# Score columns and biases from small products, and first and last six turns in an order of their own, in a two-layer graph attention kernel

## The reference

```python
Wh = jnp.matmul(h, W)                       # layer A; B has 4 heads of 128, C one of 256
e_i = jnp.einsum('bnf,f->bn', Wh, a1)
e_j = jnp.einsum('bnf,f->bn', Wh, a2)
e = jax.nn.leaky_relu(e_i[:, :, None] + e_j[:, None, :], negative_slope=ALPHA)
e = jnp.where(adj == 0, MASK_VAL, e)
attention = jax.nn.softmax(e, axis=2)
h_prime = jnp.matmul(attention, Wh)
...
x = _layernorm(x + _L0_gnn_ref(x, adj, L0_gnn_W, L0_gnn_a), axis=-1)
x = _layernorm(x + _L1_gnn_ref(adj, x, ...), axis=-1)     # layers B and C, biases b1 and b2
```

## Time and profile before

| | |
|---|---|
| median of 3 runs | 680.34 us |
| time of the profiled execution | 680.93 us |
| its span | 679.2 us |
| PE busy | 630.1 us (93%) |
| DVE busy | 598.4 us (88%) |
| ACT busy | 483.0 us (71%) |
| POOL busy | 456.0 us (67%) |
| turn 6 starts on PE | 100.84 us |
| turn 31 starts on PE | 579.33 us |

### The profile page before, as it was taken

How to read it: one execution, slowest core, us unless ns; L and a number is a source line. 1 busy time by engine, 2 the same in 40 slices (tenths; PEclk the granted TensorE clock), 3 DMA queues, 4 the chain that set the end, 5 groups by cost and what they waited for, 6 DMA issues and landing times. The chain is left out here.

```text
span 679.2 us, 17442 instructions
## 1 busy us (share of the span) xinstructions
PE 630.1 (93%) x4104; PEld 569.3 (84%) x4104; DVE 598.4 (88%) x2368; ACT 483.0 (71%) x1219; POOL 456.0 (67%) x810
## 2 busy tenths in 40 slices
PE   2468999999999999999999999999999999999883
PEld 1257889998999999889999999998999999999772
DVE  2567899999999999999999999999999999999852
ACT  1226777778777777787777777787777777787651
POOL 0125667777777777677777777777777777777742
PEclk9968999999999999999999999999999999999997
DMA  8112212112222222012222222112222222120000
GB/s 266 29 38 64 64 64 77 51 46 80 78 80 78 64 79 80 30 66 79 80 79 77 66 78 78 38 61 78 80 80 69 72 79 72 37 82 17 18 16 31
DMA packets 46868, 45.81 MB, mean 67 GB/s; under 512 B 2736, under 2 KB 46384, under 8 KB 46768
## 3 DMA queue, kind: packets, MB, share of 16 engines
q1 hardware_dynamic: 43936, 42.48, 19.6%
q10 hardware_dynamic: 2832, 2.23, 1.1%
HBM read 36.31 MB, written 8.39 MB: 66 GB/s over the span
## 5 line engine op out<-in xcount | busy, mean ns | idle before, releaser
L312 POOL TENSOR_SCALAR probB<-probB,rdenB 128x256 f32<-128x256 f32 x256 | 126.1, 505 | 74.3 <-DVE rdenB L618 73.9
L394 ACT ACTIVATE probB<-probB,shiftB 128x256 f32<-128x256 f32 x256 | 127.4, 499 | 24.2 <-DVE shiftB L587 20.7
L845 PE MATMUL PS<-probTB,VB 128*128 128x256 f32 x512 | 127.6, 382 | 0.0
L601 DVE SCALAR_TENSOR_TENSOR probB<-PS,VB,gatedB 128x256 f32<-128x256 f32 x256 | 111.5, 476 | 2.0 <-issue 0.4
L323 POOL TENSOR_TENSOR inlC<-hidT,inhC 128x512 fp32r<-128x512 f32 x64 | 82.2, 1285 | 45.0 <-ACT inhC L450 44.9
L559 DVE CUSTOM_DVE_ANT_0 gatedB<-PS,gate_bc 128x256 f32<-128x256 f32 x256 | 93.0, 417 | 7.7 <-PE PS L815 5.3
L845 PEld LDWEIGHTS PS<-probTB,VB 128*128 128x128 f32 x512 | 90.6, 192 | 8.7
L801 PE MATMUL PS<-WhB,inhB 128*128 128x260 f32 x256 | 81.6, 319 | 2.2 <-DVE inlB L632 2.1
L405 ACT ACTIVATE probTB<-PS 128x512 f32<-128x512 f32 x128 | 72.4, 591 | 8.3 <-PE PS L826 8.3
L294 POOL TENSOR_TENSOR y<-y,xres 128x512 f32<-128x512 f32 x32 | 41.2, 1288 | 51.0 <-DVE y L623 51.0
L801 PE MATMUL PS<-WhC,inhC 128*128 128x258 f32 x256 | 75.1, 293 | 0.2 <-issue 0.2
(11 more groups left out here) (98 smaller groups left out, 1631.7 us busy)
## 6 DMA issues: line engine op xcount, KB each, us to landing
xres<-in_x_dram SPq DMA_DIRECT2D x32, 256.0 KB, 2.7
xTin<-in_x_t_dram SPq DMA_DIRECT2D x32, 256.0 KB, 4.0
adj_in<-in_adj_dram SPq DMA_DIRECT2D x32, 256.0 KB, 4.3
adjT_in<-in_adj_t_dram SPq DMA_DIRECT2D x32, 256.0 KB, 3.1
out_dram<-res SPq DMA_DIRECT2D x32, 256.0 KB, 2.1
WB<-in_L_gnn_W_dram ACTq DMA_DIRECT2D x2, 256.0 KB, 5.8
WC<-in_L_gnn_W_dram ACTq DMA_DIRECT2D x1, 512.0 KB, 11.4
WA<-in_L_gnn_W_dram SPq DMA_DIRECT2D x1, 256.0 KB, 3.0
```

The lines of the kernel that those rows point to most:

```text
L312: last = pool.tensor_scalar(B.prob[h][:, k, :], B.prob[h][:, k, :], B.rden[:, k, h:h + 1], 1.0, ALU.mult, ALU.mult)
L394: last = nc.scalar.activation(L.prob[h][:, k, :], L.prob[h][:, k, :], ACT.Exp, bias=L.shift[:, k, h:h + 1], accum_out=den[:, k, h:h + 1] i ...
L601: last = nc.vector.scalar_tensor_tensor(out=L.prob[h][:, k, :], in0=PS[b][:, (h % 2) * N:(h % 2 + 1) * N], scalar=L.V[:, k, h, 1:2], in1=L ...
L845: last = nc.tensor.matmul(PS[b][:, o:o + N], B.V[:, k, h, 2:B.F + 2], B.probT[h][:, k, :], start=(k == 0), stop=(k == NT - 1))
```

## The change

Transposed copies of the three weight matrices (`WTA`, `WTB`, `WTC`), the attention vectors as 16 columns (`vectors`) and both biases as one row (`biases`) are new inputs. `scale_vectors` scales the vectors on DVE; `score_products` multiplies the transposed weights by them on PE, two result columns each (4 products for A, 8 for B, 8 for C); `score_columns` is now one copy from PSUM for each matrix. `spread_b1` and a product within `column_sums` spread the biases. `load_table` runs an exponential on one column while the inputs load, and `warm_up` four products of ones. On SP the first loads are now `WA`, the adjacency matrix, and `xTin` of batches 0 and 1; ACT loads `WTA`, the vectors, and behind `load_table` `WTB`.

Turns 0 to 5 and 31 to 36 are no longer made by `body`. Each engine has two lists, `fill` and `drain`, in which the steps of those turns stand in another order with other banks; the steps and their number are the same. `body` serves turns 6 to 30 and has only lost the one-time steps.

```diff
-def gat_kernel(nc, x, xT, adj, adjT, w0, a0, w1, asrc1, adst1, b1, w2, asrc2, adst2, b2, out):
+def gat_kernel(nc, x, xT, adj, adjT, w0, w0T, w1, w1T, w2, w2T, vectors, biases, out):
...
-        minus1 = sb("minus1", [P, 1])
...
+        minus = sb("minus", [P, P])
+        vec = sb("vec", [P, 2 * (D // P + B.H + D // P)])
+        rows = sb("rows", [1, HD + D])
...
+            L.WT = sb("WT" + L.name, [P, L.H * L.F // P, L.KT * P])
...
-            for i in range(NB + 5):
+            for i in range(6, NB + 5 - 6):
...
+            def fill():
+                b0, b1, b2, b3, b4, b5 = Turn(0), Turn(1), Turn(2), Turn(3), Turn(4), Turn(5)
+                load_weights(sp, A)
+                load_adj(b0)
+                load_xT(b0)
+                load_xT(b1)
+                load_weights_T(sp, C)
+                load_weights(sp, B)
+                load_adj(b1)
+                load_adjT(b0)
+                load_residual(b0)
+                load_weights(sp, C)
...
-            sp.dma_start(A.W[:, :, 0, 2:D + 2], w0.rearrange("(k p) f -> p k f", p=P)).then_inc(A.s_wld, DMA)
-            sp.dma_start(att0[:, :], a0.rearrange("f o -> (f o)").partition_broadcast(P)).then_inc(A.s_wld, DMA)
...
-            def load_weights():
...
-                act.dma_start(att1[:, 0, :], asrc1.rearrange("h f -> (h f)").partition_broadcast(P)).then_inc(B.s_wld, DMA)
...
-                act.dma_start(b2p[:, :], b2.partition_broadcast(P)).then_inc(C.s_wld, DMA)
+            def load_table():
+                act.wait_ge(s_cst, 6)
+                nc.scalar.activation(spare[:, :], minus[:, 0:1], ACT.Exp)
...
+            def fill():
+                b0, b1, b2, b3, b4 = Turn(0), Turn(1), Turn(2), Turn(3), Turn(4)
+                load_weights_T(act, A)
+                load_vectors(act)
+                load_table()
+                load_weights_T(act, B)
+                values(A, 1, 0, b0)
+                values(A, 0, 2, b0)
+                exp(A, 0, b0)
+                load_biases(act)
...
-            def score_columns(L, heads):
...
-                            nc.vector.scalar_tensor_tensor(out=prod[:, j, 0:L.F], in0=L.W[:, k, h, 2:L.F + 2],
-                                                           scalar=0.8 if j == 0 else -0.8, in1=v, op0=ALU.mult,
-                                                           op1=ALU.mult, accum_out=L.W[:, k, h, j:j + 1])\
-                                .then_inc(L.s_wab, 1)
...
+            def scale_vectors():
+                dve.wait_ge(s_vec, DMA)
+                v = vec[:, :].rearrange("p (n j) -> p n j", j=2)
+                for j in range(2):
+                    nc.vector.tensor_scalar(v[:, :, j], v[:, :, j], 0.8 if j == 0 else -0.8, None, ALU.mult)\
+                        .then_inc(s_vecs, 1)
+
+            def score_columns(L, b):
+                dve.wait_ge(L.s_wa, 1)
+                nc.vector.tensor_copy(L.W[:, :, :, 0:2], PS[b][:, 0:2 * L.KT * L.H]
+                                      .rearrange("p (k h j) -> p k h j", k=L.KT, h=L.H)).then_inc(L.s_wab, 1)
...
-            def finish_b1():
-                dve.wait_ge(B.s_wld, B.loads * DMA)
-                nc.vector.tensor_scalar(b1x[:, :, 2:B.F + 2], b1x[:, :, 2:B.F + 2], 1.0, None, ALU.add).then_inc(s_b1, 1)
+            def finish_b1(b):
+                dve.wait_ge(s_b1r, 1)
+                nc.vector.tensor_scalar(b1x[:, :, 2:B.F + 2], PS[b][:, 0:HD].rearrange("p (h f) -> p h f", h=B.H), 1.0,
+                                        None, ALU.add).then_inc(s_b1x, 1)
 
             def finish_b2(b):
                 dve.wait_ge(s_cs, 1)
-                dve.wait_ge(C.s_wld, C.loads * DMA)
-                nc.vector.tensor_copy(colsum[:, :], PS[b][:, 0:D + 2]).then_inc(s_fixc, 1)
-                dve.wait_ge(s_fixc, 1)
-                nc.vector.tensor_tensor(fix[:, :], colsum[:, 0:1], colsum[:, 1:2], ALU.subtract).then_inc(s_fixc, 1)
-                nc.vector.tensor_tensor(b2p[:, :], b2p[:, :], colsum[:, 2:D + 2], ALU.subtract).then_inc(s_b2, 1)
+                nc.vector.tensor_copy(b2x[:, :], PS[b][:, 0:D + 2]).then_inc(s_b2, 1)
+                dve.wait_ge(s_b2, 1)
+                nc.vector.tensor_tensor(fix[:, :], b2x[:, 1:2], b2x[:, 0:1], ALU.subtract).then_inc(s_b2, 1)
...
-            def column_sums(b, last_read):
-                pe.wait_ge(last_read, 1)
-                pe.wait_ge(C.s_wab, 2 * C.KT)
+            def score_products(L, b):
+                take_bank(b, [L.s_wab], Turn(0))
+                pe.wait_ge(s_vecs, 2)
+                pe.wait_ge(L.s_wtld, DMA)
+                first, n = {"A": (0, D // P), "B": (D // P, 1), "C": (D // P + B.H, D // P)}[L.name]
+                for k in range(L.KT):
+                    for h in range(L.H):
+                        o = 2 * (k * L.H + h)
+                        for q in range(n):
+                            v = 2 * (first + h + q)
+                            last = nc.tensor.matmul(PS[b][:, o:o + 2], L.WT[:, h + q, k * P:(k + 1) * P], vec[:, v:v + 2],
+                                                    start=(q == 0), stop=(q == n - 1))
+                last.then_inc(L.s_wa, 1)
+
+            def spread_b1(b):
+                take_bank(b, [s_b1x], Turn(0))
+                pe.wait_ge(s_rows, DMA)
+                nc.tensor.matmul(PS[b][:, 0:HD], ones[0:1, :], rows[:, 0:HD], start=True, stop=True).then_inc(s_b1r, 1)
+
+            def column_sums(b):
+                take_bank(b, [s_b2], Turn(0))
+                pe.wait_ge(s_rows, DMA)
+                pe.wait_ge(C.s_wld, DMA)
+                pe.wait_ge(C.s_wab, 1)
                 for k in range(C.KT):
-                    last = nc.tensor.matmul(PS[b][:, 0:D + 2], ones[:, :], C.W[:, k, 0, :], start=(k == 0),
+                    if k == 1:
+                        nc.tensor.matmul(PS[b][:, 2:D + 2], ones[0:1, :], rows[:, HD:HD + D], start=False, stop=False)
+                    last = nc.tensor.matmul(PS[b][:, 0:D + 2], minus[:, :], C.W[:, k, 0, :], start=(k == 0),
                                             stop=(k == C.KT - 1))
                 last.then_inc(s_cs, 1)
-                pe.wait_ge(s_fixc, 1)
+
+            def warm_up(b, count):
+                for k in range(count):
+                    nc.tensor.matmul(PS[b][:, 0:P], ones[:, :], ones[:, :], start=True, stop=True)
...
+            def fill():
+                b0, b1, b2, b3, b4 = Turn(0), Turn(1), Turn(2), Turn(3), Turn(4)
+                warm_up(7, 4)
+                score_products(A, 6)
+                project_a(1, 0, b0)
+                project_a(0, 2, b0)
```

More of the change, by code:

```diff
@@ L703, in body @@
                 values_b(0, 0, 0, t3)
-                if t3.first:
-                    finish_b2(0)
                 inverse_sum(A, 1, 3, t2)
@@ L755, in _ @@
+            nc.vector.memset(b1x[:, :, 0:2], 0.0).then_inc(s_b1z, 1)
+            fill()
             iterations(body)
+            drain()
         @block.tensor
```

963 lines of the change are left out of this document (884 added, 79 removed).

## The result

The kernel after the change takes 669.24 us, the median of four runs (667.11 to 669.67), against 680.19 us before (679.93 to 680.78): the ratio is 0.9834, with a 95% interval of 0.9821 to 0.9847. The forecast was 668.4 us. The profiled execution of the changed kernel is its shortest, 667.11 us with a span of 665.2 us, and its four runs differ by 2.6 us, so a repetition (e1) stands beside it wherever a fraction of a microsecond matters.

A forecast was written before the change was run, and what follows sets the result against it. PE, with DVE close behind, was taken to fill the 25 unchanged middle turns, leaving gains only at the ends. Start 3.0, to turn 6 6.1 and drain 3.4 sum to 12.5 us off 680.93, giving 668.4 (range 660.5 to 676.5).

The forecast's parts named there:

- the second stretch: First head maxima to turn 6: DVE sets the pace, 47.6 us of work at 93% busy, 51.2 instead of 57.26, gain 6.1.
- Loads: Start: scores wait for the adjacency matrix, landing at 6.7; first projection begins at about 9.0, 2.9 us earlier.
- Table load: Start: the 1.28 us table load, run while the inputs load, leaves the chain entirely, gaining 1.3 us.
- Scores on DVE: Start: eight `WB` score instructions leave batch 0's chain ahead of `topA`, gaining 2.1 us, less 0.4 for score C.
- The products' pace: Start: each small score MATMUL on PE takes 0.19 us, between 0.11 and 0.27.
- The charges of 4.2 us: Start, up to the x1 transposes: inserted projection costs 1.2, score B 1.6, batch 1's maxima 1.4 us.
- the rival of the fuller case: Full clock in the start (3.9), DVE 98% busy in the fill, drain filled: gain 20.3, time 660.6 us; chance 0.20.
- granted clock of 1.00 from 36 us on: Sign that the forecast holds: full granted clock from 36 us, with turn 6's first projection near 91.7.
- The sign of being wrong, DVE waits over 1 us: Middle of the fill, before turn 6: the forecast is wrong there if DVE has waits over 1 us.
- The rival by which the ends don't matter: A lead at turn 6 is lost again, so the time is 680 us; chance 0.02.
- Drain: Turn 31 to the last `weigh_head`: 5.2 us of 76.29 are empty, the new order fills two thirds, gain 3.4.
- the 95% that the prediction gave as its sign of being right: Drain: the forecast is wrong if PE is under 95% busy before the last `weigh_head`.

The follow-up runs named there:

- e1: The changed kernel run again without any edit: 668.34 us, ratio 0.9835 to the kernel before.
- e3: The changed kernel with its new order only for turns 0 to 5, turns 31 to 36 in the old order and banks: 669.95 us.
- e4: The changed kernel with the score products of C issued twice, 16 MATMULs more ahead of the transposes of `probA` of batch 0: 668.73 us.
- e5: The changed kernel without its four `warm_up` products: 668.39 us.
- e7: The changed kernel with ACT loading `WTA` and the vectors ahead of its wait for the constants: 665.09 us.
- e6: The changed kernel with twelve `warm_up` products instead of four: 667.32 us.
- e2: The changed kernel's small products and early loads, but all 37 turns in the old order and banks through `body`: 671.43 us.
- e9: e2 with the column sums of C and their copy back in turn 3, PE waiting for the copy: 679.12 us.
- e10: e7 plus twelve products of ones behind the last spread of layer C in `drain`: 666.22 us.
- e11: The kernel before the change, with 22 products of ones ahead of `transpose_x1` of batch 0: 678.76 us.

## Why the prediction was right, and which of its steps were not

The total came out because the size of the second stretch was right, the middle and tail stayed, and the error of the start (3.0 too little in this profile) and that of the drain (1.8 too much) partly cancelled. Part of that is luck. By medians the gain is 10.95 us; the profiled run alone, 13.8, flatters it, and in the profiles whose vectors landed later the start gains 3.9 to 5.4 and not 5.96. The number for the second stretch was right with a wrong cause. The steps of the start, forecast and measured:

| step | before | forecast gain | after | gain |
|---|---|---|---|---|
| first projection begins | 11.86 | 2.9 | 9.76 | 2.10 |
| from there to the spread of `VA` | 4.26 | 1.3 | 4.26 | 0.00 |
| to the transposes of `probA` | 6.14 | 1.7 | 3.86 | 2.28 |
| to the transposes of x1 | 13.89 | -4.2 | 13.24 | 0.65 |
| to the first head maxima | 7.43 | 1.3 | 6.50 | 0.93 |

**Loads.** The step said that the scores would wait for SP's second load, landing at 6.7. The adjacency matrix was there before 4.31; what came late was the 8 KB of vectors, to which no landing time had been given. The time came out close (9.0 and 9.76), the reason was wrong, and in four other profiles with the same loads (e1, e3, e4, e5) it is 10.59 to 11.37. e7 shows the cost: about 3 us of the median.

**Table load, 1.3 forecast, 0 measured.** The row at 14.02 in the earlier trace rows was taken as holding up the first copy of values. It did, but the copy that the spread waits for is that of the second tile, whose projection ran until 15.64, beyond the end of the table load at 15.30. Before, the spread came 4.26 us behind the first projection; this is its row in the kernel before:

```profile
16.12 0.69 PE L815 MATMUL PS<-ident,VA 128*128 128x128 f32 x2 [0.48 <-ACT VA L384]
```

After, it stands at 14.02 behind 9.76, the same 4.26 us. The step lay beside other work.

**Scores on DVE, 2.1 less 0.4 forecast, 2.3 measured.** This step held. Score C ran right up to the transposes (14.50 + 3.41 = 17.91, transposes at 17.88), as said.

**The products' pace.** 0.19 us a MATMUL was taken, between 0.11 and 0.27. It is 0.23 (score A, 1.87 for 8) and 0.21 (score C) at the low clock and 0.115 (score B) at the full one: all lie between the bounds, and the sum of 7.1 us is near the 7.5 forecast. e4 shows that even doubling one set moves the time by 0.4.

**The charges of 4.2 us: this step of the start failed.** 1.2 for the projection put ahead of `weigh`, 1.6 for score B and 1.4 for the maxima of batch 1 were each worked out with the paces of the old start. But the same inserted rows kept PE at work, with no gap like the old 5.45 and 5.83 us, and the clock rose at 21.6 us, where it had risen at 27.3 before: `weigh(A)` took 2.48 instead of 3.61 and score B 1.84 instead of 3.4. Instead of costing 4.2 the path to x1 became 0.65 shorter, and between 0.1 and 0.8 shorter in e1, e3, e5 and e7. e6 shows that the clock did it: with the same order at the low clock for most of this path it is 16.78, 2.9 longer than before. What raised the clock is less clear. In e2 and e9, in the old order, the small products fill most or all of the gap of 5.45 too, and `weigh(A)` still ran at the low clock, which rose only at 26.1 and 27.7. The charge and the clock had been weighed as separate questions, the clock only from 40 us on. In this place the rival of the fuller case was the better description; its start of 3.9 was reached or passed in the profiles (3.9 to 5.96). The sign "granted clock of 1.00 from 36 us on" held in the profile of the kernel after and not in e1, where the clock was low from 46.0 to 52.8.

The Trainium skill ("TensorE: Matmul & The Clock Gate", Part 1) says that activity releases the throttle. The rows agree: e6's 24 MATMULs of ones give the full clock to what follows, and behind the four products of the kernel after the next rows run at the low one, as the prediction assumed (e5 without them: 668.39, e1 with them: 668.34). That sentence of the page does not speak against a short burst by itself, though, as the prediction has it; e5 does.

**First head maxima to turn 6: the right number for the wrong reason.** 51.2 us were forecast from 47.6 us of DVE work at 93%; it is 51.34 from 46.26 at 90%. The work was 1.3 too much, the fullness 3 points too high. The reason given was the new order, with two or three batches to choose from, and the round trip of `finish_b2` came last in that sentence. e2 and e9 turn this round: moving the round trip is worth 5.05 us, the order at most 1.2. The sign of being wrong, DVE waits over 1 us, was met (1.3 for `inhB`) although the number was right. In the earlier trace rows the round trip was a wait of 2.1 us, one of several, which is why I did not price it by itself. Its price is the wait, plus DVE's second wait behind it, plus what PE held back meanwhile.

**Middle.** 478.5 forecast, 478.26 measured, and no experiment moved it beyond 477.9 to 478.4. The rival by which the ends don't matter is out.

**Drain, 3.4 forecast, 1.64 measured.** The term that failed is the empty time. 5.2 us were found as the length less PE's work by paces, and two thirds of it taken. The idle time in the earlier trace rows is only 76.29 - 73.32 = 2.97, of which two thirds would be 2.0; the working by paces had left out 2.3 us for which PE counts as busy. In the kernel after 74.65 - 73.44 = 1.21 us of idle time are left, so the order took 1.76 of 2.97 us out, and the drain became 1.64 shorter. The share of two thirds was thus nearly right (59%), and the time that it was taken of was not. (More moved at the end than the two steps named under "The change": the last transposes of `probB` too stand two products of the last heads earlier than before.) The largest idle time left on PE in the drain of the kernel after is this:

```profile
585.97 0.36 PE L1480 MATMUL PS<-WhB,inhB 128*128 128x260 f32 x1 [0.64 <-DVE inlB L972]
```

PE is busy for 98% of the drain by the profile, well above the 95% that the prediction gave as its sign of being right. The sign was met and the gain was not: it was too weak a sign, as before the change PE was at 96% already.

**Tail.** 23.6 forecast, 23.33 measured, with the last `weigh` at the low clock as before. In one run of e10 the tail is 21.41, 1.9 less, with the last `weigh` at the full clock; over four runs that gain is not established.

## What to carry to other kernels

A one-time step that goes from one in-order queue to another and back should be priced as a ring, by taking it out: its wait row said 2.1 us here, and moving it was worth 5. Issue the first loads ahead of every wait of the engine that issues them, even a small load of 8 KB, since its landing may set the whole start (3.3 us between e5 and e7); then a lead of the start passes undiminished through a middle that PE fills. And before a removed step is counted as a gain, look for what else the next step waits for: the table load of 1.28 us was worth nothing.

The fastest version found is e7 (the changed kernel with its two first ACT loads issued earlier): 665.09 us, 0.9785 [0.9769, 0.9802] of the kernel before.

## What the runs showed of the hardware

Float32 products with a full 128x128 weight load and only two columns took 0.21 to 0.23 us a MATMUL at the granted clock of 1.2 GHz and 0.115 at 2.4 GHz, which is nearly what a transpose with 128 columns costs (0.11 at full clock in the earlier trace rows). The products of ones, with 128 columns, took 0.118 a MATMUL at the full clock (24 in 2.84 us in e10). Two columns were no cheaper than 128.

An 8 KB load took 4.0 to 4.2 us from issue to landing in the five profiles in which ACT issued it ahead of its wait (at 1.31 us in e7), and 4.8 to 6.2 in the six in which it was issued 1.2 us later, behind four loads of SP and one of ACT; the time differed from run to run.

Raising the clock early did not keep it up. In e6 score C at 11.90 ran at the full clock, `weigh(A)` at 17.84 at the low one, score B at 21.19 at the full one and the column sums at 27.14 at the low one again. In the kernel after it rose near 21 us and was low again only from 31.9 to 35.3. In the kernel after the fall came behind 0.89 us of idle time of PE (up to 31.12), in e6 the two falls, at 14.3 and 24.5, came within idle times of 1.50 and 0.52 us; whether the idle time causes the fall, and how much of it is too much, was not tested. In e11 the granted clock is at 0.50 from 38.0 to 41.4 us, behind the waits at the x1 transposes, although PE had been kept at work up to them.
